# Three fp32r passes for an fp32 product: the first products of the gated expert layer

## What is computed

```python
gate_logits = x @ Wg + bg
top_vals, top_idx = jax.lax.top_k(gate_logits, 2)          # of 8 experts
w = jax.nn.softmax(top_vals, axis=-1)
h = jnp.einsum('td,edh->eth', xf, W0) + b0[:, None, :]     # d = 128, h = 512
g = jax.nn.silu(jnp.einsum('td,edh->eth', xf, W1) + b1[:, None, :])
y = jnp.einsum('eth,ehd->etd', h * g, W2) + b2[:, None, :]
out = jnp.einsum('te,etd->td', combine, y)
```

## Time and profile before

| | us |
|---|---|
| median of 3 runs (lowest to highest) | 1168.18 (1164.74 to 1171.41) |
| profiled execution, its own time | 1163.98 |
| its span in the trace | 1162.2 |
| PE busy | 1032.4 (89%) |
| DVE busy | 718.2 (62%) |
| ACT busy | 644.3 (55%) |
| POOL busy | 573.0 (49%) |

### The profile page before, as it was taken

The page is one execution under the profiler, slowest core; times in us unless marked ns, Lnnn a source line. Parts: engine busy times, 40 slices in busy tenths (PEclk is TensorE's granted clock), DMA queues, the critical chain, the costliest instruction groups (busy, mean ns, idle before and its releaser), DMA issues.

```text
span 1162.2 us, 22081 instructions
## 1 busy us (share of the span) xinstructions
PE 1032.4 (89%) x6754; PEld 777.6 (67%) x6754; DVE 718.2 (62%) x2446; ACT 644.3 (55%) x2117; POOL 573.0 (49%) x926
## 2 busy tenths in 40 slices
PE   4977999968899998969999998888799999978995
PEld 3864889835555566856777765677567776745995
DVE  5476345476767684277776777533876676772454
ACT  2335333447788834448887876243387888752231
POOL 5232765443000033558564666767475555666452
PEclk9987999989999999999999999698799999996997
DMA  3003556697900114120000000275300000004666
GB/s 66 13 26 98 176 168 202 202 169 301 351 1 2 38 51 132 55 66 20 2 19 1 19 2 19 66 219 158 92 19 2 2 1 2 2 26 143 203 211 197
DMA packets 116004, 102.85 MB, mean 88 GB/s; under 512 B 18027, under 2 KB 97571, under 8 KB 115888
## 3 DMA queue, kind: packets, MB, share of 16 engines
q1 hardware_dynamic: 105280, 82.71, 24.0%
q0 software_dynamic: 8448, 17.20, 4.4%
q10 hardware_dynamic: 2160, 1.53, 0.5%
HBM read 65.04 MB, written 36.36 MB: 87 GB/s over the span
## 4 chain that ended last, share of the span: by engine, by line
PE 60%; DVE 15%; POOL 7%; issue 6%; ACT 5%; DMA 5%; SPq 2%; DVEq 0%; POOLq 0%; ACTq 0%
PE ps L2977 5%; PE ps L2781 4%; PE ps L2783 4%; PE ps L2782 4%; PE ps L2991 4%; PE ps L2873 4%; PE ps L2886 3%; PE ps L3519 3%; PE ps L3523 3%; PE ps L3172 3%; PE ps L3532 2%; PE ps L3005 2%; PE ps L3331 2%; ACT ex L1325 2%; PE ps L3320 2%
## 5 line engine op out<-in xcount | busy, mean ns | idle before, releaser
L1325 ACT ACTIVATE ex<-ps,nmx 128x154 f32<-128x154 f32 x512 | 194.0, 391 | 74.7 <-DVE nmx L2282 72.9
L1087 POOL TENSOR_TENSOR pp<-ex,rc 128x256 f32<-128x256 f32 x256 | 157.6, 616 | 145.9 <-DVE rc L2287 145.1
L2282 DVE TENSOR_REDUCE nmx<-ps 128x2 f32<-128x308 f32 x256 | 119.5, 470 | 60.2 <-PE ps L2783 59.4
L2977 PEld LDWEIGHTS ps<-ident,pp 128*128 128x128 f32 x640 | 74.5, 143 | 55.5 <-POOL pp L1088 45.8
L2781 PE MATMUL ps<-kp,q_s 128*128 128x308 f32 x256 | 96.1, 375 | 14.0 <-ACT ex L1325 11.4
L1325 ACT ACTIVATION_READ_ACCUMULATOR ex<-ps,nmx 128x1 f32 x512 | 105.1, 205 | 0.0
L2977 PE MATMUL ps<-ident,pp 128*128 128x128 f32 x640 | 101.3, 283 | 2.5 <-POOL pp L1088 1.9
L1442 ACT ACTIVATE pe<-ps,nmx 128x154 f32<-128x154 f32 x256 | 84.9, 394 | 32.0 <-DVE nmx L2165 30.9
L924 POOL DMA_INDIRECT yq_d<-yq,ids_q x78 | 74.7, 957 | 54.3 <-DVE yq L2034 35.4
L2782 PE MATMUL ps<-kp,q_s 128*128 128x308 f32 x256 | 79.8, 312 | 0.0
L2783 PE MATMUL ps<-kp,q_s 128*128 128x308 f32 x256 | 79.8, 312 | 0.0
(11 more groups left out here) (483 smaller groups left out, 2727.0 us busy)
## 6 DMA issues: line engine op xcount, KB each, us to landing
w_r<-in_L_ffn_W SPq DMA_DIRECT2D x69, 256.0 KB, 3.4
xq_d<-blankq SPq DMA_DIRECT2D x4, 4160.0 KB, 23.9
w_q<-in_L_ffn_W SPq DMA_DIRECT2D x46, 256.0 KB
w_q<-in_L_ffn_w SPq DMA_DIRECT2D x46, 128.0 KB
xq<-xq_d SPq DMA_DIRECT2D x24, 130.0 KB, 3.2
w_s<-in_L_ffn_W SPq DMA_DIRECT2D x8, 256.0 KB
w_e<-in_L_ffn_W SPq DMA_DIRECT2D x8, 256.0 KB, 5.1
acc<-yq_d SPq DMA_DIRECT2D x8, 256.0 KB, 4.4
```

Of the source, the lines that this page charges most:

```text
L1087: pool.tensor_tensor(pp[st % 2][:, m % 4, 2 * j:2 * j + 2, :], w[:, :, 0:P], r.broadcast_to([P, 2, P]), ALU.mult)
L1325: ins = act.activation(ex[:, tt % NEX, j, :], ps[:, tt % 3, j * SK:(j + 1) * SK], ACT.Exp, bias=nmx8[:, tt % 8, j:j + 1], accum_out=sm8[:, ...
L2282: dve.tensor_reduce(nmx8[:, tt % 8, :], ps[:, tt % 3, 0:2 * SK].rearrange("p (h s) -> p h s", h=2), AX.X, ALU.max, negate=True).then_inc(n ...
L2977: last = pe.transpose(ps[:, bank, k * P:(k + 1) * P], pp[st % 2][:, k, c, :], ident[:, :])
```

## The change

In the 16 pair runs each first product becomes three fp32r passes. For that, both operands are split on chip. ACT writes the high part of the columns (xc_hi, in columns) and of both weights (w_hi, new function high_weights); the type fp32r rounds on writing. DVE subtracts to get the low parts: w1_lo and w0_lo in place over the raw weights (low_weights), and xc_lo out of PSUM (low_columns). hidden_run of a pair waits for all of them, and columns waits until low_columns has read the PSUM bank that it writes. The W2 load gets semaphores of its own, so hidden_run no longer waits for it and down_run does. Singles keep fp32.

```diff
+        s_w2, w2_from = [in_x, in_vec, in_ffn], [16 * B, 16 * 9, 16 * 13]
+        s_wh, s_wl, s_xl = z_rc, z_hc, z_eb
...
                     u = k % NW
                     wait(sp, s_yp, k - NW + 1)
-                    sp.dma_start(w2_r[u][:, :, :], ...).then_inc(s_wr[u], 16)
+                    sp.dma_start(w2_r[u][:, :, :], ...).then_inc(s_w2[u], 16)
...
                     act.wait_ge(s_xp, k + 1)
                     wait(act, s_h, 2 * (k - 1))
-                    act.activation(xc_r[k % 2][:, 0:P * TALL[k]], ps[:, 4, 0:P * TALL[k]], ACT.Identity).then_inc(s_x, 1)
+                    into = xc_hi if TALL[k] == 2 else xc_r
+                    act.activation(into[k % 2][:, 0:P * TALL[k]], ps[:, 4, 0:P * TALL[k]], ACT.Identity).then_inc(s_x, 1)
+
+                def high_weights(k):
+
+                    if k >= PAIRS:
+                        return
+                    act.wait_ge(s_wr[k % NW], 32 * (k // NW + 1))
+                    wait(act, s_h, 2 * (k - 1))
+                    act.activation(w_hi[k % 2][0][:, :], w1_r[k % NW][:, :], ACT.Identity).then_inc(s_wh, 1)
+                    act.activation(w_hi[k % 2][1][:, :], w0_r[k % NW][:, :], ACT.Identity).then_inc(s_wh, 1)
...
+                high_weights(0)
                 columns(0)
+                high_weights(1)
                 columns(1)
                 for k in range(NRUN):
                     gates(k, 0)
                     gates(k, 1)
+                    high_weights(k + 2)
                     if 2 <= k < 2 + B:
                         turned(k - 2)
                     if k + 2 < NRUN:
                         columns(k + 2)
...
+                def low_weights(k):
+
+                    if k >= PAIRS:
+                        return
+                    for n, (raw, lo) in enumerate(((w1_r, w1_lo), (w0_r, w0_lo))):
+                        dve.wait_ge(s_wh, B + 2 * k + n + 1)
+                        ins = dve.tensor_tensor(lo[k % NW][:, :], raw[k % NW][:, :], w_hi[k % 2][n][:, :].bitcast(F32), ALU.subtract)
+                    ins.then_inc(s_wl, 1)
+
+                def low_columns(k):
+
+                    if k >= PAIRS:
+                        return
+                    dve.wait_ge(s_x, k + 1)
+                    wait(dve, s_h, 2 * (k - 1))
+                    dve.tensor_tensor(xc_lo[k % 2][:, :], ps[:, 4, 0:RUN], xc_hi[k % 2][:, :].bitcast(F32), ALU.subtract).then_inc(s_xl, 1)
...
+                low_columns(0)
+                low_weights(0)
+                low_columns(1)
+                low_weights(1)
                 products(0, 0)
                 products(0, 1)
                 for k in range(NRUN):
+                    low_weights(k + 2)
                     if k + 1 < NRUN:
                         products(k + 1, 0)
                         products(k + 1, 1)
+                    low_columns(k + 2)
                     weigh(k)
...
                     wait(pe, s_x, k)
+                    if k:
+                        pe.wait_ge(s_xl, B + min(k, PAIRS))
                     for h in range(TALL[k]):
                         last = pe.transpose(ps[:, 4, h * P:(h + 1) * P], xr[k % NXG][:, h, :], ident[:, :])
...
+                def first_product(bank, k, n, cols):
+
+                    if TALL[k] == 2:
+                        return product(bank, (w_hi[k % 2][n][:, cols], (w1_lo, w0_lo)[n][k % NW][:, cols]), (xc_hi[k % 2][:, :], xc_lo[k % 2][:, :]))
+                    return mm(bank, (w1_r, w0_r)[n][k % NW][:, cols], xc_r[k % 2][:, 0:P], start=True, stop=True)
+
                 def hidden_run(k):
 
-                    pe.wait_ge(s_wr[k % NW], 48 * (k // NW + 1))
+                    pe.wait_ge(s_wr[k % NW], 32 * (k // NW + 1))
                     pe.wait_ge(s_x, k + 1)
+                    if TALL[k] == 2:
+                        pe.wait_ge(s_wl, B + k + 1)
+                        pe.wait_ge(s_xl, B + k + 1)
...
                 def down_run(k):
 
+                    pe.wait_ge(s_w2[k % NW], w2_from[k % NW] + 16 * (k // NW + 1))
                     pe.wait_ge(s_hd, 2 * k + 2)
```

More of the change, by code:

```diff
@@ L355, in xattn_moe_stack @@
         w2_r = [over(f"w2_r{u}", [P, 4, D], F32, (arena_at + 30336, arena_at + 36480, w1_at + 6144)[u])[0] for u in range(NW)]
+        w1_lo = [at(f"w1_lo{u}", [P, 4 * P], F32R, 26240 + 6144 * u) for u in range(NW)]
+        w0_lo = [at(f"w0_lo{u}", [P, 4 * P], F32R, (28288, 34432, 12352)[u]) for u in range(NW)]
+        w_hi = [[at(f"w_hi{u}{n}", [P, 4 * P], F32R, 56832 + 4096 * u + 2048 * n) for n in range(2)] for u in range(2)]
+        xc_hi = [over(f"xc_hi{u}", [P, RUN], F32R, pt_at + 12288 + 1024 * u)[0] for u in range(2)]
+        xc_lo = [at(f"xc_lo{u}", [P, RUN], F32R, 74240 + 1024 * u) for u in range(2)]
         h_r = [over(f"h_r{u}", [P, 4, RUN], F32, pt_at + 4096 * u)[0] for u in range(2)]
@@ L777, in last_weights @@
                     wait(sp, s_yp, k - NW + 1)
-                    sp.dma_start(w2_r[u][:, :, :], t[f["w2"]][bass.ds(e, 1)].rearrange("a (c p) d -> p (a c) d", p=P)).then_inc(s_wr[u], 16)
+                    sp.dma_start(w2_r[u][:, :, :], t[f["w2"]][bass.ds(e, 1)].rearrange("a (c p) d -> p (a c) d", p=P)).then_inc(s_w2[u], 16)
                 for b in range(B):
@@ L3518, in hidden_run @@
                         for c in range(2):
-                            last = mm(ps[:, G % 2, c * RUN:c * RUN + P * TALL[k]], w1_r[k % NW][:, (2 * q + c) * P:(2 * q + c + 1) * P], xc_r[k % 2][:, 0:P * TALL[k]], start=True, stop=True)
+                            last = first_product(ps[:, G % 2, c * RUN:c * RUN + P * TALL[k]], k, 0, slice((2 * q + c) * P, (2 * q + c + 1) * P))
                         last.then_inc(s_g, 1)
@@ L3522, in hidden_run @@
                         for c in range(2):
-                            last = mm(ps[:, 2 + G % 2, c * RUN:c * RUN + P * TALL[k]], w0_r[k % NW][:, (2 * q + c) * P:(2 * q + c + 1) * P], xc_r[k % 2][:, 0:P * TALL[k]], start=True, stop=True)
+                            last = first_product(ps[:, 2 + G % 2, c * RUN:c * RUN + P * TALL[k]], k, 1, slice((2 * q + c) * P, (2 * q + c + 1) * P))
                         last.then_inc(s_h, 1)
                 def down_run(k):
+                    pe.wait_ge(s_w2[k % NW], w2_from[k % NW] + 16 * (k // NW + 1))
                     pe.wait_ge(s_hd, 2 * k + 2)
```

## The result

The median went from 1168.35 to 1182.05 us (1176.22 to 1182.84). The ratio is 1.0101, with a 95% interval from 1.0073 to 1.0129: slower by 11.8 us, with 8.5 and 15.1 as bounds (the medians lie 13.7 apart). The predicted sum was 12.0, the predicted time 1180.

What follows compares the result with a forecast made beforehand. It took TensorE to bound the pair runs. The terms 11.7 + 1.6 + 0.6 - 0.9 - 1.0 gave +12.0 us, on the median of 1168.18 a time of 1180, range 1169 to 1193.

Steps and rivals of the forecast that it cites:

- The mechanism: Pair runs: column copy, gates and products form one chain from the transposes; low_columns stands behind it and hidden_run waits.
- The recurrence: Pair runs: the delay recurs in 14 cycles, hidden_run(2) to hidden_run(15), and cannot be worked off.
- The cycle: Pair run, transposes to next transposes: 6.72 us instead of 5.46; 0.5 saved lost to 1.77 of standing.
- The bias products: Pair cycles with turn and bias_out products: these fit into TensorE's new standing time.
- Run 4: Pair run where low_context, replicate_columns, add_bias and a mask meet on DVE: products 1.6 us too late, +1.6.
- The clock: Rival: TensorE's standing in each cycle drops its clock to 1.2 GHz; 1221 us, half of them 1200; chance 0.08.
- Late weights: ACT waits in high_weights for weight loads, columns queued behind: +0.6 us, kept at 0 to 2.5.
- The single runs: The start of run 18 no longer waits for the W2 load: -0.9 us, nothing if another load is late.
- The first two runs: hidden_run(0) and (1) gain without the new wait, their splits done while gathers are awaited: -1.0 us.
- The main term: 14 cycles from the transposes of run 2 to those of run 16: 94.1 us against 82.41, 11.7 more.
- TensorE-bound: Rival: TensorE stays the bound in the pair runs and gets faster, cycle 4.95 us, time 1159; chance 0.06.
- Faster passes: Rival: hidden_run's 24 passes at about 0.105 us or less, near 1171; a gain below 0.083; chance 0.06.

Runs made afterwards that it cites:

- experiment 1: The changed kernel with low_columns moved ahead of the products in DVE's list: 1163.38 us, ratio 0.9965 to the kernel before.
- experiment 3: The kernel before (fp32 products, no weight splits) plus only low_columns behind products and hidden_run waiting for it: 1188.75 us, one execution.
- Experiment 2: The changed kernel without low_weights, the third pass using the high part of the weights: 1178.17 us, one execution.
- experiment 8: The changed kernel with only low_context and replicate_columns moved from their old place to two later runs: 1178.92 us, one execution.
- run 18: Not a follow-up: a single run inside the kernel; in the kernel before its start waited 0.89 us for loads, W2 the last issued.
- experiment 6: On top of experiment 1: masks split over three runs each, their loads moved, low_context and replicate_columns moved to later runs: 1155.03 us, ratio 0.9900.
- run 2: Not a follow-up: a pair run inside the kernel, the first whose hidden_run meets the new wait; its transposes begin the 14 cycles.
- run 16: Not a follow-up: the run inside the kernel after the 16 pair runs; its transposes end the 14 cycles.
- experiment 4: The changed kernel without low_weights, low_columns and their waits, all three passes on high parts: 1166.55 us, ratio 0.9982 to the kernel before.
- run 15: Not a follow-up: the last pair run inside the kernel; its cycle in the high-parts-only kernel took 8.42 us.

## Why the prediction was right, and where its terms were off

**The mechanism.** One chain from the transposes through column copy, gates and products, with low_columns at its end and TensorE waiting for it: the cycle shows it, experiment 1 removes it, experiment 3 has it alone. Experiment 2 rules out the weights' splits as its cause. The recurrence holds too: 14 waits.

**The cycle, 6.72 forecast, 6.74 measured.** low_columns started at T+3.14, exactly as weigh had. It took 0.41 for 0.42. From its end to TensorE's first load passed 0.23 us (200.43 to 200.66) where the earlier trace rows had given 0.11, and 0.03 more to the first pass. From there to the next transposes went 2.93, where 2.95 for the passes and 0.10 for the stall had been put: 24 passes at the measured 0.119 are 2.86, and the first interval (200.69 to 200.88) is 0.07 longer than the others. So +0.12 and +0.03 against -0.12 and -0.01.

The formula for a warm matmul in the Trainium skill, "TensorE: Matmul & The Clock Gate", section "Back-to-back issue gap", gives an estimate of 0.109 us a pass here; the measured 0.119 decides against it, as the neighbouring rows had.

**The bias products** disappeared into the standing time as forecast: of the four cycles of 6.7 to 6.8 us that had them before, two are 6.74 or 6.75 now. The other two are the slow cycle and the one behind it, and in experiment 8 they are 6.74 too.

**Run 4, +1.6 forecast, +2.84 measured, and 0.15 in the next cycle.** The DVE part was nearly right: the first pass starts 1.45 us later than usual (T+5.26 for T+3.81). The other 1.39 is the clock, which the prediction held as a rival for all or half of the cycles and not for this one alone; its tail makes the cycle of 6.89, whose transposes still ran slowly, so that the column copy starts at T+0.55 (163.59) and not at T+0.41. This is the largest mis-sized term. Its lesson is that a rival can come true in a single cycle.

**Late weights, +0.6 forecast, nothing measured.** ACT waited three times, up to 4.93 us, in time that was free anyway: none of the 14 cycles is longer for it.

**The single runs, -0.9 forecast, -0.37 measured.** The W2 wait of run 18 went, as said. But the last mask's work was not placed against it. The timeline of DVE and TensorE in run 18's cycle, which begins at 224.52:
```profile
225.15 0.80 DVE L1837 TENSOR_TENSOR mask_bf<-mask_f,row_neg 128x616 bf16<-128x616 f32 x1
...
225.99 1.13 DVE L2650 SCALAR_TENSOR_TENSOR h_r<-ps,bias_r,g_r 128x128 f32<-128x128 f32 x4
...
226.65 0.71 PE L3560 MATMUL ps<-xc_r,w_r 128*128 128x128 f32 x4 [0.20 <-DVE h_r L2650]
```
TensorE now meets the mask on DVE and waits 0.20 us for the products behind it. The cycle of run 18 takes 3.57 us instead of 3.95; the cycles after it take 3.24. In experiment 6, where this mask's work is in other runs, TensorE does not wait there and run 18's cycle takes 3.30. The earlier trace rows showed the stall and what caused it, not what came next in line.

**The first two runs, -1.0 forecast, -1.45 measured** from the first gather to run 2's transposes. Eight groups of six passes, 0.715 us each at 0.119 a pass instead of 0.865, explain 8 x 0.15 = 1.2. The same stretch wanders with the gathers (1.3 to 2.8 us under the kernel before in the other kernels with passes, and equal to it in experiment 3, which has none), so the rest isn't explained.

**Sum:** +14.95 in the pairs, -1.45 before, -0.47 from run 16's transposes to the end of the stage, +13.0; forecast were +13.9, -1.0 and -0.9. The main term, 11.7 for the 14 cycles, is earned: experiment 8 has 12.0. Among the smaller ones the clock in run 4's cycle was left out and the W2 stall counted too high, while late weights were priced at 0.6 for nothing and the first two runs gained more than forecast. These misses nearly cancelled, so that the number was nearer than its parts is luck.

**Rivals.** TensorE-bound: false as built, true of the usual cycle after one moved line. Faster passes: false, at 0.119 us; and by the prediction's own sum the break-even was near 0.09 us a pass, not 0.083. The clock: true in one cycle of 14, and at a lower price than forecast: the slow passes stood 0.21 us apart, which makes 24 of them 5.1 us and not 5.9.

## What to carry to other kernels

When a bound engine gets a new operand from another engine, look up in that engine's own order what stands ahead of the producer, and whether that hangs on the same event: 0.4 us of work put behind such a chain cost 1.9 us in each usual cycle, and in such a cycle nothing ahead of it. Cheaper work on the bound engine uses up everyone else's slack, so list who is next (here the mask ahead of the weights in SP's queue, then DVE's pile of preparations in one run) and mend these too, or the gain stays on paper: against the kernel before, one moved line gave 0.35%, the queues and piles the rest of 1.0%. A mean of busy shares shows neither; one cycle of the timeline and the table of waits do.

## What the runs showed of the hardware

The clock's fall does not follow from the length of one wait alone. It fell to the 1.2 GHz level (passes 0.21 us apart instead of 0.12) after 2.04 us of standing in the changed kernel, 2.30 in experiment 4 and 1.50 in experiment 2; it stayed at 1.00 through 1.64 us in each of eight cycles of the changed kernel, through 1.73 in one of experiment 1 and through 3.18 us in one cycle of experiment 4, that of run 15:
```profile
199.56 0.35 PE L2818 MATMUL ps<-xc_hi,w_hi 128*128 128x256 f32 x1 [3.18 <-ACT g_r L1617]
```
```profile
194.22:202.64 8.42, 5.24 (x44) 5.00 (x43) 2.06 (x6) 2.88 (x7) 2.85 (x4) 1.00 0.73 248
```
The Trainium skill, "TensorE: Matmul & The Clock Gate", section "A second HAM failure mode: psum-queue depth-cycling", tells of throttling from frequent short idle times; the regular 1.64 us of the changed kernel's cycles did not bring it about. Single waits of 1.50 to 2.30 us did, though not each wait of that length or longer. What tells them apart was not tried. The passes of such a hidden_run took 4.32, 4.59 and 4.44 us instead of 2.93, and those of the next were back at full clock.

A wait of TensorE for a DVE result ended 0.23 us after the result here, where the earlier trace rows had shown 0.11 us for another pair of instructions: a single row is a thin base for such a price.
